# One decoder layer on one core: attention and cross stage put in one block, groups 0 and 1 of the cross stage run beside the attention's last pairs, buffers laid out anew

## The reference, cut to what matters

```python
x = x + attn(layernorm(x))     # 16 heads of 16, each token looks at itself and 7 earlier ones, 8 apart;
                               # weights rounded to -1, 0, 1; bias by distance; softmax; out @ wo.T
x = x + xattn(layernorm(x))    # 64 context rows per batch entry: scores = coef * (x Wq) . ctx,
                               # all but the 54 largest of 64 masked, softmax, weighted context @ W_o.T
x = x + ffn(layernorm(x))      # shared expert for every token, and of 16 routed experts the 4 that
                               # sigmoid(gate_w x) + gate_b picks: silu(h1 * h2) @ w2, weighted and summed
```

## Time and profile before

| | us |
|---|---|
| median of 3 runs (784.65 to 788.28) | 786.47 |
| the profiled execution | 783.57 |
| its span, first to last instruction | 781.8 |
| attention's last `add` ends | 198.5 |
| first indirect scatter issued | 255.68 |
| last indirect scatter issued | 466.66 |
| first load of the expert phase | 472.00 |

### The profile page before, as it was taken

How to read it: one execution, slowest core, us unless ns; L and a number is a source line. 1 busy time by engine, 2 the same in 40 slices (tenths; PEclk the granted TensorE clock), 3 DMA queues, 4 the chain that set the end, 5 groups by cost and what they waited for, 6 DMA issues and landing times. The chain is left out here.

```text
span 781.8 us, 15783 instructions
## 1 busy us (share of the span) xinstructions
PE 628.4 (80%) x4034; PEld 543.3 (69%) x4034; DVE 569.3 (73%) x1747; ACT 417.7 (53%) x1136; POOL 457.8 (59%) x363
## 2 busy tenths in 40 slices
PE   0888769969238899999774506999999999999994
PEld 0676758757236566665542305899999999999993
DVE  5799967991476877776646715988888888888883
ACT  3886436421235646545431305766666666666662
POOL 3457593645000544556665660677777776877875
PEclk9989999999668999999975757999999999999997
DMA  9910001030330566543334623678888887888984
GB/s 293 295 57 28 29 13 41 28 109 28 128 128 31 193 231 227 183 185 118 126 133 149 208 106 99 108 131 138 148 141 139 138 144 124 144 144 135 148 131 58
DMA packets 77095, 100.38 MB, mean 128 GB/s; under 512 B 9745, under 2 KB 70305, under 8 KB 76449
## 3 DMA queue, kind: packets, MB, share of 16 engines
q0 software_dynamic: 26736, 37.64, 26.5%
q1 hardware_dynamic: 48096, 59.64, 25.2%
q10 hardware_dynamic: 2176, 2.10, 0.9%
HBM read 50.97 MB, written 52.95 MB: 133 GB/s over the span
## 5 line engine op out<-in xcount | busy, mean ns | idle before, releaser
L1562 POOL DMA_INDIRECT out_dram<-yw,xg x143 | 222.1, 1553 | 87.8 <-issue 53.7
L1184 POOL DMA_INDIRECT xs_scratch<-rows,slot x128 | 125.7, 982 | 138.2 <-DMA xs_scratch<-rows,slot 77.8
L1445 PE MATMUL cbank<-w,stc_hi 112*128 (+1 forms) x572 | 110.2, 286 | 0.9 <-DVE stc_hi L1527 0.9
L1445 PE MATMUL cbank<-w_hi,xtc_hi 128*128 x286 | 105.2, 368 | 2.2 <-DVE xtc_lo L1457 1.7
L355 POOL TENSOR_TENSOR pv<-v_sb,pr 128x256 f32<-128x256 f32 (+7 forms) x32 | 68.5, 2155 | 57.3 <-DVE pr L344 39.8
L1445 PEld LDWEIGHTS cbank<-w,stc_hi 112*128 112x128 f32 (+1 forms) x572 | 93.4, 189 | 2.2 <-issue 1.7
L1445 PE MATMUL cbank<-w,xtc_hi 128*128 x286 | 93.1, 326 | 0.0
L1445 PE MATMUL cbank<-w_hi,xtc_lo 128*128 x286 | 92.3, 323 | 0.0
L1434 PE MATMUL cbank<-identb,xg 128*128 128x128 f32 x286 | 55.4, 276 | 30.5 <-DMA xg<-xs_scratch 30.5
L1499 DVE TENSOR_TENSOR hh<-cbank,h 128x176 f32<-128x176 f32 x143 | 48.8, 341 | 42.1 <-ACT h L1493 42.1
L1505 ACT ACTIVATE sgc<-hh 128x128 f32<-128x128 f32 x143 | 44.4, 310 | 60.8 <-DVE hh L1499 60.3
(11 more groups left out here) (223 smaller groups left out, 1542.8 us busy)
## 6 DMA issues: line engine op xcount, KB each, us to landing
xg<-xs_scratch SPq DMA_DIRECT2D x143, 144.0 KB, 2.8
w<-w13r_dram SPq DMA_DIRECT2D x8, 704.0 KB, 6.2
w_hi<-ctx_t_dram SPq DMA_DIRECT2D x8, 512.0 KB, 4.4
x_scratch<-x_all SPq DMA_DIRECT2D x16, 256.0 KB, 2.1
w_hi<-x_scratch SPq DMA_DIRECT2D x8, 512.0 KB, 4.2
out_dram<-w SPq DMA_DIRECT2D x16, 256.0 KB
w<-w2r_dram SPq DMA_DIRECT2D x4, 1024.0 KB, 9.4
x_all<-x_dram SPq DMA_DIRECT2D x12, 256.0 KB, 8.2
```

The source lines that it names most:

```text
L1184: nc.gpsimd.indirect_dma_start(t["xs"], bass.IndirectOffsetOnAxis(ap=slot[:, n % 2, k:k + 1].bitcast(U32), axis=0), rows[:, n % NROW, k // ...
L1445: last = nc.tensor.matmul(out, stationary, moving, start=j == 0, stop=j == len(pairs) - 1)
L1562: nc.gpsimd.indirect_dma_start(t["out"], bass.IndirectOffsetOnAxis(ap=xg[:, p, ID:ID + 1].bitcast(U32), axis=0), yw[:, p % YB, :], None, c ...
```

## The change

Attention and the cross stage become two parts of one block (`attention_part`, `cross_part`, joined in `front_phase`). The barrier between them, and the clearing of semaphores there, is gone. Attention runs as before through turn 16 (`FIRST_LEFT = WIN + 9`). For what comes then a written-out list, `passage`, gives each of PE, ACT, DVE and POOL its steps in order, the attention's last pairs (8 to 15) mixed with the first steps of groups 0 to 6. After the list `cross.run` goes on with the old table and leaves out what is done. POOL has only `values` 12 to 15 in its list and then the scatters.

The eight PSUM banks are shared: `R[0:2]` of the cross stage are `ps_qk`, `R[4:6]` are `ps_q`, `R[2]`, `R[3]` are `ps_t`, `ps_p`, and `R[6]`, `R[7]` are `ps_v`, `ps_s`; the first user of each waits for attention's last reader. `x_all` is split in `x_first` (pairs 0 to 7) and `x_second`. The places of the expert weights still lie over attention's buffers; so their loads come behind the store of the last pair. `cross_at` and `cross_bp` are gone as such: the same products are now `at_mm`, `bp_mm` of groups 0 and 1. The clearing of `rows`, `prt`, `hsr` goes from POOL to DVE. The rows of groups 0 to 2 are loaded after store 8 (before: after store 10). The identity matrix is loaded once less.

```diff
+def front_phase(nc, t, keep, outer):
...
+        R = [ps_qk[:, 0, :], ps_qk[:, 1, :], ps_t, ps_p, ps_q[:, 0, :], ps_q[:, 1, :], ps_v, ps_s]
...
+        passage = dict(g=" ".join(f"values:{j}" for j in range(12, PAIRS)))
...
+            stA:0 add:9 root:0 scores:14 add:10 weigh:13 scores:15 weigh:14 zeros:0 negs:0 add:11 tops:0 weigh:15 masks:0
...
+        FIRST_LEFT = WIN + 9
+        done = set(sum(passage.values(), []))
+
+        def turn(eng, who):
+            att.run(eng, who, 0, FIRST_LEFT)
+            for what, n in passage[who]:
+                what(eng, n)
+            cross.run(eng, who, done)
...
+            for j in range(WIN + 1):
+                att.store(eng, j)
+            att.first_rows_stored(eng)
+            for n in range(NX1):
+                pre.load_x1(eng, t, n)
+            for j in range(WIN + 1, PAIRS):
+                att.store(eng, j)
+                if j == PAIRS - 3:
+                    cross.load_ct(eng, 2)
+                if j == PAIRS - 2:
+                    cross.load_x1(eng, NX1)
+                    cross.load_ct(eng, 3)
+            att.rows_stored(eng)
+            cross.table_load(eng)
+            for i in range(NG + LAST):
+                cross.sync_turn(eng, i)
```

```diff
         def sc_mm(eng, n):
 
             f["at_ev"].wait(eng, n)
             f["tA_ev"].wait(eng, n)
             f["x2"].wait(eng, n - 1)
+            if n == 0:
+                att.queries_read(eng)
```

More of the change, by code:

```diff
@@ L675 @@
 class CrossInputs:
-    LOADS = 19
+    LOADS = 18
     ZEROS = 3
@@ L1295, in split_lo @@
-        def split_lo(experts):
-            def go(eng, n):
-                if n == NG - 1:
-                    for e in experts:
-                        eng.wait_ge(keep["s_hi"], e + 1)
-                        nc.vector.tensor_tensor(keep["w13"].bitcast(R32)[:, :, e, :], keep["w13"][:, :, e, :],
-                                                keep["w13_hi"][:, :, e, :].bitcast(F32), ALU.subtract).then_inc(keep["s_lo"], 1)
-            return go
-        order = dict(
-            t=[(1, sc_mm), (2, t_c), (3, sh_mm), (1, p_t), (0, t_a), (1, y_mm), (2, rest_mm), (0, at_mm(1)), (2, l_t),
-               (0, at_mm(0)), (0, bp_mm), (2, rk_mm), (3, ys_mm(0)), (3, ys_mm(1)), (2, table_mm)],
-            v=[(1, negs), (1, tops), (1, masks), (-1, stA), (3, split_lo(range(0, 4))), (1, x2_), (1, stC),
-               (-1, root, NG + 2), (2, choose), (3, hs_), (3, split_lo(range(4, 7))), (2, shares), (2, spread), (2, hsr_),
-               (3, xf_(0)), (3, xf_(1)), (2, table), (3, split_lo(range(7, NE)))],
-            s=[(1, expo), (2, t_c_ev), (1, p_t_ev), (0, t_a_ev), (3, g1_), (2, th_), (0, at_ev), (2, g1r_), (1, xhC),
-               (-1, xhA), (0, bp_ev), (2, split_hi(range(0, 7))), (3, split_hi(range(7, NE)))],
-            g=[(3, scatter(2)), (3, scatter(3)), (2, scatter(0)), (2, scatter(1))])
@@ new lines, in front_phase @@
+        cross = cross_part(nc, t, keep, R, lambda name, shape, dt=F32: ctx.enter_context(nc.sbuf_tensor(name, shape, dt)), sem,
+                           flow, att)
+        ops = {**att.ops, **cross.ops}
+        passage = dict(g=" ".join(f"values:{j}" for j in range(12, PAIRS)))
+        passage["t"] = """
+            out_t:11 qkv:15 proj:10 at_1:0 at_0:0 out_t:12 bp_mm:0 t_a:0 at_1:1 at_0:1 sc_mm:0 out_t:13 bp_mm:1 proj:11
+            proj:12 out_t:14 p_t:0 y_mm:0 proj:13 t_a:1 proj:14 out_t:15 sc_mm:1 proj:15 t_c:0 p_t:1 rest_mm:0 l_t:0 t_a:2
+            y_mm:1 rk_mm:0 at_1:2 at_0:2 sc_mm:2 bp_mm:2 sh_mm:0 p_t:2 t_c:1 t_a:3 y_mm:2 at_1:3 at_0:3 rest_mm:1 sc_mm:3
+            l_t:1 bp_mm:3 rk_mm:1 ys_0:0 ys_1:0 t_c:2 sh_mm:1 rest_mm:2 p_t:3 t_a:4 l_t:2 y_mm:3 at_1:4 at_0:4 ys_0:1
+            ys_1:1 rk_mm:2 bp_mm:4
@@ new lines, in front_phase @@
+        """
+        passage["v"] = """
+            stA:0 add:9 root:0 scores:14 add:10 weigh:13 scores:15 weigh:14 zeros:0 negs:0 add:11 tops:0 weigh:15 masks:0
+            stA:1 add:12 root:1 x2_:0 add:13 stC:0 stA:2 add:14 root:2 negs:1 tops:1 masks:1 add:15 stA:3 choose:0
+            shares:0 spread:0 x2_:1 stC:1 negs:2 root:3 tops:2 masks:2 hsr_:0 x2_:2 hs_:0 stC:2 stA:4 choose:1 root:4
+            shares:1 spread:1 hsr_:1 xf_0:0 xf_1:0 negs:3 tops:3 masks:3 stA:5 hs_:1 choose:2 shares:2 x2_:3 stC:3 hsr_:2
+            root:5 spread:2 xf_0:1 xf_1:1 negs:4 tops:4 masks:4 stA:6 x2_:4 stC:4 root:6
@@ L1354, in _ @@
-            run(eng, "g")
+            att.start["g"](eng)
+            att.run(eng, "g", 0, FIRST_LEFT)
+            for what, n in passage["g"]:
+                what(eng, n)
+            eng.wait_ge(pre.s_pad, 16 * pre.ZEROS)
+            cross.run(eng, "g", done)
         @block.scalar
         def _(eng):
-            eng.wait_ge(s_init, 3)
-            run(eng, "s")
+            att.start["s"](eng)
+            turn(eng, "s")
         @block.vector
         def _(eng):
-            eng.wait_ge(s_init, 3)
```

1813 lines of the change are left out of this document (911 added, 902 removed).

## The result

The changed kernel takes 759.3 us (median of 4 runs, 757.04 to 759.45); the kernel before took 787.4 beside it (784.65 to 788.54). The ratio is 0.965, 95% interval 0.962 to 0.968: faster by 28 us. Forecast were 763 us, with 747 to 778 as the range. The profiled executions are 783.57 us before and 759.45 after, 24.1 apart; their spans are 781.8 and 757.6.

A forecast was written before the change was run, and what follows sets the result against it. Bound: POOL's scatters, each waiting for a landing, whose start sets the end. First scatter 26.7 us earlier, chain 5.0 longer: 783.57 - 26.7 + 5.0 = 761.9, median put 1 above at 763; range 747 to 778.

The forecast's parts named there:

- Step 1: On DVE after turn 16: stA and root of group 0 4.5 us, add of pair 9 0.7, waiting for POOL 2.0.
- Step 2: On DVE: scores 14, weigh 13, add 10 in 10.6 us, then scores 15 and weigh 14 in 11.2, to 180.0.
- Step 3: On DVE: the clearing, 1.0 us taken from 0.3 to 1.7, then negs of group 0, 0.9, to 181.9.
- Steps 4 and 5: On DVE: addition 11 at 184.2, tops and weigh 15 to 188.3; masks, waiting for POOL's last values, through at 196.2.
- The price of that wait: Rival on DVE beside POOL's value products: no port wait of size, first scatter 6.4 us earlier, 756.5 us; chance 0.14.
- Step 6: On DVE after masks of group 0: stA, add, root, x2_ and stC work through the second root, 196.2 to 211.2.
- Step 7: On DVE: negs of group 1 waits for PE's sc_mm until 213.1; negs, tops, masks, add and stA end at 220.4.
- Step 8: Choose waits for PE until about 222, then choose to spread 6.6 us, POOL 1.1 later: 229.8.
- The chain: POOL's scatters, first to last: one more pair of weight pieces beside them, 5.0 us longer, between 0 and 10.0.
- Entangled lists: Rival: one late step in the hand-written lists holds four engines; first scatter at 245, 778 us; chance 0.14.
- Only the barrier: Rival: the groups' steps still wait for attention's end, so only 5.2 us are removed; 783 us; chance 0.03.
- The scatters never finding their calm half: Rival: loads and stores spread out, all groups run at 32.8 us, chain 262, time 807 us; chance 0.05.

The follow-up runs named there:

- masks first: The changed kernel with masks of group 0 ahead of weigh of pair 15 in DVE's order: 757.7 us, ratio 0.963 to the kernel before.
- unmixed lists: The changed kernel with its lists rewritten so attention's last pairs finish before group 0 starts, still without a barrier: 779.9 us, ratio 0.990 to the kernel before.

## Why the prediction was right

- **The bound and the walk to it.** The end moved with the first scatter less the chain's growth: forecast 26.7 - 5.0 = 21.7 earlier, measured 28.7 - 4.7 = 24.1 (rounded). In the clock of its own profile after is 759.45 where 761.9 was the sum. From the end of turn 16 to the first scatter it took 77.1 us for some 78; the other 1.0 is an earlier start. Single steps were off by up to 1.7 us either way and partly cancelled, and the first scatter moves by 4 us from run to run, so the closeness is in part luck.
- **Start, steps 1 and 2.** Turn 16 ended at 149.9 for 150.9. Step 1 took 7.0 us for 7.2, with a port wait of 2.0 as forecast: 1.6 at L831 (1.75 for 0.16) and 0.4 at L781 (0.60 for 0.17), each to the end of a POOL instruction. But both are TENSOR_SCALARs with one tile, and the forecast had the steps with two inputs wait. Step 2 took 22.0 for 21.9.
- **Step 3.** The clearing took 1.8 us (178.91 to 180.74), over its bound of 1.7, and 1.0 was taken. Each piece is 0.04 or 0.05 us shorter than on POOL, but gaps lie between them.
- **Steps 4 and 5.** Addition 11 at 182.36 for 183.5; masks through at 194.4 for 196.2. The full wait of 3.4 us twice is there. The Trainium skill (SBUF — State Buffer, "Who interferes with whom") has it that a DVE instruction with two SBUF inputs blocks for the whole of a GpSimd instruction that reads SBUF; the trace agrees for masks, 3.72 and 3.70 us. That the wait is not for such instructions alone is what step 1 and masks first show.
- **The price of that wait was not settled.** The forecast gave 6.4 us to its absence. Masks first moved the wait to two other instructions and gained 1.1 us at most; taking root away from it too lost 1.4 to 1.8 against that, by PE. There only 1.7 us of the 7.1 were left as a wait on DVE, and attention's end came no earlier than in after. No kernel here ran without the wait and with all else in place, so the 6.4 is neither shown nor refuted.
- **Step 6** took 16.1 for 15.0: DVE waited 0.73 and 0.77 us for PE, which stood at 1.2 GHz (granted clock 0.50 from 192 to 200) after its 6.21 us of waiting for masks. **Step 7** took 7.5 for 9.2: sc_mm of group 1 ran at 2.4 GHz (granted clock 1.00 from 205 to 213; 1.20 us for 32 matmuls, 2.00 at 1.2 GHz in the row it was priced by the earlier trace rows) and negs did not wait for it. That eight pieces of PE were priced at 1.2 GHz is wrong: out_t of pair 15 took 3.66 us at a granted clock of 1.00 and proj 1.99, as in the rows of before, which were at 1.00 already (189.43 to 194.8). What gained was sc_mm, 0.8 us, and t_a, 1.04 for 2.0. **Step 8** took 8.9 for 9.4. The 1 us that I took off for PE was 2 in these two steps.
- **The chain: right sum, wrong working.** 4.7 us for 5.0. But the 5.0 was to come from four pieces beside group 0, whose length stayed (31.2 for 31.1); it came in group 1, 6.3 us more, less the 2.5 us that groups 3 to 7 won. Four pieces go out within group 1 now, for two before, and 6.2 us of its 39.1 went when none did; that the two more make the growth fits this, but was not tried by itself. And the 20 us that the first groups had over the calm ones were put down to the pieces, 5.0 a pair. With the pieces out of the way, the three first ones still took 90.5 us, some 20 over the calm pace, 3.8 of it the wait for slots. By the runs a pair costs 1.5 us (8.7 over six; 2.1 with those 3.8 counted) to 4.2. The forecast of the chain, 5.0, was right by luck, then: the price a pair was too high and the place wrong.
- **Rivals.** Entangled lists: in after nothing of it, 245 was its first scatter; moving one step, root, made PE wait 2.0 us more. Only the barrier: the unmixed lists gave 779.9 us, for the 783 of the prediction. The scatters never finding their calm half: did not come, groups 3 to 7 took 22.4 to 23.7.
- **Signs.** All within their bounds: no group's first scatter waited for its slots, and the last add ended at 215.95. Group 0 took over 31 us, but no longer than before; group 1 did.

## What to carry to other kernels

Find the chain that the end hangs on and ask what starts it: here work was worth 20 us not because it got shorter, but because it was put into waits of 8 us that another stage left open. Before moving one instruction out of another's way, look at who waits for it on the other engines; of two edits made to save 7 us on DVE one gained at most 1.1 and the other nothing. A gain from more transfers in flight has to be measured on more than one chip: the same program was 6.4% faster than the kernel before on one and 1.2% slower on another.

## What the runs showed of the hardware

- A TENSOR_SCALAR with one tile of 128 x 4 waits for POOL's product as well (1.75, 1.89 and 3.06 us for 0.17 alone). BATCH_NORM over SBUF (1.40), an addition of PSUM and SBUF (0.74), and x2_ with PSUM (1.66) kept their length beside it.
- Bulk loads on SP's queue delay POOL's scatters: twelve weight pieces moved beside groups 5 and 6 made these 15.9 us longer (62.9 for 46.9), three pairs beside groups 3 to 5 made them 6.6 to 12.7 us longer.
- Chips of one kind differ in stalls that the trace does not explain: with three scatters in flight 733.8 to 737.7 us on one chip, 795.5 to 802.3 on another.
